# Moving a piece of layer 1, half of layer 2 and half of the dense part around the last tile's products in a recommender tower

## The chip, the cores and the metric

The kernel runs on one core of one Trainium2 chip. A core has TensorE (matmuls; PE in the profile, its weight loads PEld), VectorE (DVE), ScalarE (ACT), GpSimd (POOL) and SyncE (SP), and 16 DMA engines that all of them share. The metric is the time of one execution on the device in microseconds (us), the median of several runs: 106.18 us before, from 106.04 to 106.2 in 3 runs.

## What is computed

512 samples, 26 embedding tables with rows of 128 floats, and 128 dense features per sample. For each sample the 27 vectors (dense and 26 looked up) are multiplied with each other, the 351 products above the diagonal go with the dense features (twice) into a small network of three layers. All numbers are float32.

```
e = stack([tbl_f[ids[:, f]] for f in range(26)], axis=1)          # 512 x 26 x 128
x = concatenate([dense[:, None, :], e], axis=1)                   # 512 x 27 x 128
g = einsum('bnd,bmd->bnm', x, x)[:, triu_i, triu_j]               # 512 x 351
h = concatenate([dense, g, dense], axis=1)                        # 512 x 607
h = maximum(h @ W_top1 + b_top1, 0)                               # 512
h = maximum(h @ W_top2 + b_top2, 0)                               # 256
y = h @ W_top3                                                    # 1
```

## The kernel before

The samples are worked on in four tiles of 128. The order of the work on each engine is written out by hand, and each engine goes through its list in order and waits on semaphores; nothing is scheduled by a tool.

Eleven small tables are looked up by matmul with one-hot rows (`lookup`, L334): DVE and ACT make the one-hot rows and split the tables in two parts, and the table rows come by DMA from SP. The other 15 tables are gathered by POOL with indirect DMAs (L307), 15 for each tile in groups of 4, 4, 4 and 3, so 60 in all and groups 0 to 15. PE turns each group (`turn_group`, L349) into `ps_rows`, and ACT copies it into `xt` (`copy_group`, L659). The last group of the last tile is group 15. A gather waits, besides for the ring of rows, for lookups that are done (L306), the last of these waits being that for all 13 lookups.

A tile's products are `gram(t, quarter)` (L371): four quarters, each with 32 matmuls of 27x27 in the program. Every float32 matmul stands twice in the trace, each time as a weight load and a matmul, so that one quarter is 64 pairs of records, `layer1_pairs(t, m)` 6 pairs, half of `layer2` 8, half of `layer1_dense` 4. The first quarter waits until ACT has copied the tile's groups. After the last quarter DVE turns the blocks and packs them (`pack`, L587 and L592), PE turns the packed products (`turn_z`, `turn_last_z`), ACT copies them, and then come layer 1 (`layer1_pairs`, L420; of the last tile `layer1_last_pairs`, L397), relu on ACT and DVE, layer 2 (L434, L447), relu, and layer 3 (L460).

Tiles are overlapped: the quarters of tile 1 stand between pieces of layers 1 and 2 of tile 0, those of tile 2 between pieces of tile 1. Around the fourth tile (t = 3) the order is another: all of layer 1 of tile 2, the turn of group 14, half of layer 2 of tile 2, the turn of group 15 (the last turn), half of the dense part of tile 3 (L410), the four quarters in a row, and then the other half of layer 2 and of the dense part, while DVE packs.

The lines that matter are L512 to L540 of the list on PE, `gram` (L353), `layer1_pairs` (L413), `layer2` (L425), `layer1_dense` (L402), on ACT `relu1_low(2)`, `copy_group(14)` and `copy_group(15)` (L734 to L736).

Of the kernel before, what the change touches and what calls it, by code (L numbers as in the profile page):

```python
# [25 lines left out]
M1, M2 = H1 // P, H2 // P  # L26
# [95 lines left out]
def build(nc, dense_by_column, ids, ids_by_table, tables, w1, w2, columns, identity, out):  # L122
    with ExitStack() as ctx:
# [100 lines left out]
        def h1_block(t, m):  # L224

            return ps_a[:, m // 2, (m % 2) * P:(m % 2 + 1) * P]

        def h2_block(t, m):

            if t == TILES - 1:  # L230
                return ps_rows[:, m, 0:P]
            return ps_h2[:, 0, m * P:(m + 1) * P]
# [80 lines left out]
        def _(pe):  # L313
# [26 lines left out]
            def turn_group(g):  # L340

                t, first, n = GROUPS[g]
                if g >= 2:
                    pe.wait_ge(group_copied, g - 1)
                if g == 0:
                    pe.wait_ge(ident_landed, 16)
                pe.wait_ge(group_landed[g], 16 * n)
                for slot in range(n):
                    last = pe.transpose(ps_rows[:, g % 2, slot * P:(slot + 1) * P],  # L349
                                        rows_sb[:, t % ROWS_RING, first + slot, :], ident)  # L350
                last.then_inc(group_turned, 1)

            def gram(t, quarter):  # L353

                half, first = divmod(quarter * SPQ, SPB)
                if quarter == 0:

                    pe.wait_ge(group_copied, GROUPS_UP_TO[t])  # L360
                    pe.wait_ge(lookup_copied, FIRST_HALF_UP_TO if t < TILES // 2 else len(LOOKUPS))
                    if t == 0:
                        pe.wait_ge(dense_copied, 1)
                        pe.wait_ge(gram_zeroed, 1)
                    else:
                        pe.wait_ge(blocks_turned, t)
                for s in range(first, first + SPQ):
                    for j in range(P // NPAD):
                        b = t * P + j * NPAD + half * SPB + s
                        x = xt[:, b // RUN, :, b % RUN]  # L370
                        last = pe.matmul(ps_gram[j * NPAD:j * NPAD + N, half, s * N:(s + 1) * N], x, x,  # L371
                                         start=True, stop=True)
                if quarter == QUARTERS - 1:
                    last.then_inc(gram_done, 1)
# [27 lines left out]
            def layer1_dense(t, k):  # L402

                if k == 0 and t == 0:
                    pe.wait_ge(w1d_summed, 1)
                    pe.wait_ge(lookup_copied, len(LOOKUPS))
                if t:
                    pe.wait_ge(h1_high_ready if k else h1_low_ready, t)
                for m in range(2 * k, 2 * k + 2):
                    pe.matmul(h1_block(t, m), w1d[:, m * P:(m + 1) * P],  # L410
                              dense_sb[:, t * P:(t + 1) * P], start=(m % 2 == 0), stop=False, skip_group_check=True)

            def layer1_pairs(t, m):  # L413

                if m == 0:
                    if t == 0:
                        pe.wait_ge(w1_landed, 16)
                    pe.wait_ge(z_copied, t + 1)
                for c in range(ZC):
                    last = pe.matmul(h1_block(t, m), w1_sb[:, c, m * P:(m + 1) * P],  # L420
                                     zt[:, t % 2, c, :], start=False, stop=(c == ZC - 1), skip_group_check=True)
                if m % 2:
                    last.then_inc(h1_done, 1)

            def layer2(t, half):  # L425

                if half == 0:
                    pe.wait_ge(layers_landed, 32)
                    if t:
                        pe.wait_ge(h2_ready, M2 * t)  # L430
                pe.wait_ge(h1_high_ready if half else h1_low_ready, t + 1)
                for k in range(half * M1 // 2, (half + 1) * M1 // 2):
                    for m in range(M2):
                        last = pe.matmul(h2_block(t, m), w2_sb[:, k, m * P:(m + 1) * P], h1[:, t % 2, k, :],  # L434
                                         start=(k == 0 and m == 0), stop=(k == M1 - 1), skip_group_check=True)
                if half:
                    last.then_inc(h2_done, 1)
# [80 lines left out]
            turn_z(2)  # L518
            turn_group(13)

            for m in range(M1):
                layer1_pairs(2, m)
            turn_group(14)
            layer2(2, 0)
            turn_group(15)
            layer1_dense(3, 0)
            gram(3, 0)
            gram(3, 1)
            gram(3, 2)
            gram(3, 3)  # L530
            layer2(2, 1)
# [244 lines left out]
```

## Time and profile before

| | |
|---|---|
| median of 3 runs | 106.18 us (106.04 to 106.2) |
| span of the profiled execution | 141.4 us (the profile gives no other time for it) |
| PE busy | 105.4 us, 75% of the span |
| DVE, ACT, POOL busy | 52.7, 48.3, 60.9 us |
| "issue" in the chain that ended last | 23% of the span |
| mean granted TensorE clock | 0.855 of full speed |

The profiled execution is 35.2 us longer than the median of the runs. Most of that is idle time of PE that the profile puts down to "issue": the engine waited for nothing that the profile shows. It lies mainly between 51 and 99 us from the start of the span. From 102 us on the engine works at its pace, but for one gap.

In the rows below a timeline line is: start in us, length in us, engine, line of the kernel, operation, tile written <- tile read, form, number of records, and in brackets the idle time before them and what ended it. Lengths of matmuls are modelled at their end, so the difference of two starts is the better measure of a pace.

### The profile page before, as it was taken

Reading aid. Unit: us, or ns where it says so; the run is one execution under the profiler, and the core shown is the slowest. Engines: PE = TensorE matmul, PEld = TensorE weight load, DVE = VectorE, ACT = ScalarE, POOL = GpSimd, SP = SyncE. Lnnn points to the kernel's source line nnn. Section 1 sums busy time; section 2 is a strip of 40 time slices with the busy share of each in tenths; the row PEclk is TensorE's granted clock in tenths of the full one; section 3 lists DMA queues with packets and bytes.
Section 4 is the critical chain, followed back from the end, with each engine's and each line's share of the span. In section 5 each row is a group of like instructions: output and inputs, shape, how many; then the busy total and the mean of one; then the engine's idle time right before and its main releaser. Section 6 shows DMA issues by size and latency. Waiting matters only on the chain.

```text
span 141.4 us, 3474 instructions
## 1 busy us (share of the span) xinstructions
PE 105.4 (75%) x1525; PEld 85.9 (61%) x1525; DVE 52.7 (37%) x116; ACT 48.3 (34%) x82; POOL 60.9 (43%) x66
## 2 busy tenths in 40 slices
PE   6999899999979960366795223441997999967993
PEld 2476678788858950164684122221996998957980
DVE  2999999699279800000050000000043034103210
ACT  4749929597079520201023000000105106310342
POOL 1887877478567775705227777770000000000000
PEclk9999999999999997558689555555599999998699
DMA  4899999999992122100101122220000000000000
GB/s 131 282 234 256 264 262 234 249 241 234 305 381 71 51 60 55 38 19 23 37 5 48 48 59 57 56 56 19 0 5 5 5 5 0 0 5 5 5 0 1
DMA packets 5365, 13.46 MB, mean 95 GB/s; under 512 B 1731, under 2 KB 1991, under 8 KB 5222
## 3 DMA queue, kind: packets, MB, share of 16 engines
q1 hardware_dynamic: 3260, 9.11, 24.1%
q0 software_dynamic: 1920, 3.94, 10.8%
q8 instruction: 12, 0.20, 0.6%
q10 hardware_dynamic: 170, 0.18, 0.4%
q14 instruction: 3, 0.02, 0.0%
HBM read 13.23 MB, written 0.00 MB: 94 GB/s over the span
## 4 chain that ended last, share of the span: by engine, by line
PE 65%; issue 23%; DVE 6%; ACT 2%; DMA 2%; DVEq 0%
PE ps_a L334 27%; PE ps_gram L371 11%; PE ps_a L420 9%; DVE onehot L560 5%; PE ps_h L434 5%; PE ps_rows L349 4%; PE ps_a L410 3%; PE ps_a L397 2%; DMA idrow<-ids_by_table 2%; PE ps_rows L447 1%; ACT xt L659 1%; DVE part_sb L569 1%; PE ps_h L460 1%; ACT table_sb L666 1%; PE ps_gram L390 0%
## 5 line engine op out<-in xcount | busy, mean ns | idle before, releaser
L307 POOL DMA_INDIRECT rows_sb<-tbl,ids_sb x60 | 60.5, 1009 | 34.1 <-issue 16.5
L334 PE MATMUL ps_a<-onehot,part_sb 125*128 125x512 f32 (+1 forms) x208 | 46.9, 376 | 2.9 <-issue 2.6
L334 PEld LDWEIGHTS ps_a<-onehot,part_sb 125*128 125x128 f32 x208 | 35.8, 197 | 11.2 <-issue 3.4
L371 PE MATMUL ps_gram<-xt 128*27 128x27 f32 x1024 | 16.9, 205 | 22.5 <-issue 21.6
L371 PEld LDWEIGHTS ps_gram<-xt 128*27 128x27 f32 x1024 | 13.5, 118 | 27.1 <-issue 25.1
L560 DVE TENSOR_SCALAR onehot<-idrow,row_id 125x1024 fp32r<-125x1024 int16 (+1 forms) x42 | 27.7, 712 | 4.9 <-remote 3.3
L608 DVE TENSOR_SCALAR table_sb<-ps_a,columns_sb 128x128 f32<-128x128 f32 x8 | 2.4, 347 | 43.7 <-PE ps_a L420 39.5
L420 PE MATMUL ps_a<-table_sb,w_sb 128*128 128x128 f32 x72 | 13.0, 326 | 6.8 <-issue 6.4
L652 ACT COPY xt<-ps_a 128x512 f32<-128x512 f32 (+1 forms) x13 | 7.5, 575 | 31.1 <-PE ps_a L334 18.9
L587 DVE STREAM_TRANSPOSE table_sb<-ps_gram 128x864 f32<-128x864 f32 x4 | 4.3, 1084 | 32.3 <-PE ps_gram L371 32.3
L420 PEld LDWEIGHTS ps_a<-table_sb,w_sb 128*128 128x128 f32 x72 | 11.2, 232 | 7.6 <-issue 6.9
L569 DVE TENSOR_TENSOR part_sb<-table_sb,part_sb 125x512 fp32r<-125x512 f32 x22 | 14.5, 682 | 1.5 <-ACT part_sb L631 1.5
L631 ACT CAST part_sb<-table_sb 125x1024 fp32r<-125x1024 f32 (+1 forms) x12 | 11.7, 984 | 3.0 <-DMA table_sb<-tbl 2.9
L682 ACT ACTIVATE table_sb<-ps_a,columns_sb 128x128 f32<-128x128 f32 x8 | 2.5, 364 | 29.4 <-remote 23.5
L659 ACT COPY xt<-ps_rows 128x512 f32<-128x512 f32 (+1 forms) x16 | 9.7, 607 | 3.9 <-PE ps_rows L349 3.2
L349 PE MATMUL ps_rows<-ident_sb,rows_sb 128*128 128x128 f32 x60 | 9.2, 272 | 0.0
L689 ACT ACTIVATE table_sb<-ps_h,columns_sb 128x128 f32<-128x128 f32 x6 | 1.9, 364 | 17.9 <-PE ps_h L434 17.9
L349 PEld LDWEIGHTS ps_rows<-ident_sb,rows_sb 128*128 128x128 f32 x60 | 7.2, 140 | 0.8
L434 PE MATMUL ps_h<-table_sb,w_sb 128*128 128x128 f32 x48 | 7.5, 303 | 0.0
L641 ACT ACTIVATE distance<-idrow,row_id 125x1024 f32<-125x1024 int16 (+1 forms) x6 | 6.5, 1085 | 0.3 <-DMA idrow<-ids_by_table 0.3
L468 PE MATMUL ps_z<-zeros 128*128 128x512 bf16 x13 | 5.7, 629 | 1.2 <-DVE zeros L544 1.2
L434 PEld LDWEIGHTS ps_h<-table_sb,w_sb 128*128 128x128 f32 x48 | 6.3, 205 | 0.2
(35 smaller groups left out, 46.0 us busy)
## 6 DMA issues: line engine op xcount, KB each, us to landing
table_sb<-tbl SPq DMA_DIRECT2D x11, 448.0 KB
idrow<-ids_by_table SPq DMA_DIRECT2D x5, 256.0 KB
w_sb<-w SPq DMA_DIRECT2D x1, 1280.0 KB, 8.7
rows_sb<-tbl,ids_sb POOLq DMA_INDIRECT x60
table_sb<-tbl SPq DMA_DIRECT2D x10, 52.0 KB
w_sb<-w SPq DMA_DIRECT2D x1, 512.0 KB
dense_sb<-dense_by_column SPq DMA_DIRECT2D x1, 256.0 KB
idrow<-ids_by_table ACTq DMA_DIRECT2D x1, 128.0 KB
```

Source lines behind the costliest of these rows:

```text
L307: pool.indirect_dma_start(rows_sb[:, t % ROWS_RING, k, :], None, tables[f], bass.IndirectOffsetOnAxis(ids_sb[:, t, f:f + 1], 0),).then_inc ...
L334: last = pe.matmul(ps_a[:, i % 2, a:b], parts_sb[part][:, w, c * D:(c + 1) * D], unit_onehot(u, c)[:, member, a:b], start=(part == HIGH an ...
L349: last = pe.transpose(ps_rows[:, g % 2, slot * P:(slot + 1) * P], rows_sb[:, t % ROWS_RING, first + slot, :], ident)
L371: last = pe.matmul(ps_gram[j * NPAD:j * NPAD + N, half, s * N:(s + 1) * N], x, x, start=True, stop=True)
L420: last = pe.matmul(h1_block(t, m), w1_sb[:, c, m * P:(m + 1) * P], zt[:, t % 2, c, :], start=False, stop=(c == ZC - 1), skip_group_check=True)
L434: last = pe.matmul(h2_block(t, m), w2_sb[:, k, m * P:(m + 1) * P], h1[:, t % 2, k, :], start=(k == 0 and m == 0), stop=(k == M1 - 1), skip ...
L560: dve.tensor_scalar(unit_onehot(u, c), idrow[0:VP, w, 0:n, :], row_id[0:VP, first + c:first + c + 1], None, ALU.is_equal).then_inc(onehot_ ...
L569: dve.tensor_tensor(parts_sb[LOW][:, w, columns], table_sb[0:VP, s, columns], parts_sb[HIGH][:, w, columns].bitcast(F32), ALU.subtract).th ...
L631: act.copy(parts_sb[HIGH][:, w, first:end], table_sb[0:VP, s, first:end]).then_inc(part_ready[HIGH], 1)
L641: act.activation(distance[:, 0:n, :], idrow[0:VP, w, 0:n, :], ACT.Abs, bias=row_id[0:VP, negated:negated + 1]) \
L652: act.copy(xt[:, a // RUN:b // RUN, 1 + h, :], ps_a[:, i % 2, a:b].rearrange("p (q r) -> p q r", r=RUN)).then_inc(lookup_copied, 1)
L659: act.copy(xt[:, t * P // RUN:(t + 1) * P // RUN, slots, :].rearrange("p q n r -> p n q r"), ps_rows[:, g % 2, 0:n * P].rearrange("p (n q ...
```

## The change

The change reorders the list of PE and nothing else; ACT, DVE, POOL and SP go through the same instructions. Layer 1 of tile 2 is cut: its first two pieces stand where they were, the third stands between the turns of groups 14 and 15, and the fourth behind the last turn. The first half of layer 2 of tile 2 and of the dense part of tile 3 stand between the second and the third quarter of tile 3's products; they stood ahead of and behind the last turn.

```
-            for m in range(M1):
-                layer1_pairs(2, m)
+            layer1_pairs(2, 0)
+            layer1_pairs(2, 1)
             turn_group(14)
-            layer2(2, 0)
+            layer1_pairs(2, 2)
             turn_group(15)
-            layer1_dense(3, 0)
+            layer1_pairs(2, 3)
             gram(3, 0)
             gram(3, 1)
+            layer2(2, 0)
+            layer1_dense(3, 0)
             gram(3, 2)
             gram(3, 3)
             layer2(2, 1)
```

On PE, from the turn of group 13 to that of group 15 (L349: turns of a group; L420: layer 1 of tile 2, `w1_sb` its weights; counts are the program's, half of the trace's):

```order
 L349 MATMUL ps_rows<-ident_sb,rows_sb 128x128 x4
-L420 MATMUL ps_a<-table_sb,w1_sb 128x128 x12
+L420 MATMUL ps_a<-table_sb,w1_sb 128x128 x6
 L349 MATMUL ps_rows<-ident_sb,rows_sb 128x128 x4
+L420 MATMUL ps_a<-table_sb,w1_sb 128x128 x3
+L349 MATMUL ps_rows<-ident_sb,rows_sb 128x128 x3
+L420 MATMUL ps_a<-table_sb,w1_sb 128x128 x3
```

The last turn (x3) has 9 matmuls of layer 1 ahead of it instead of 12, and 3 behind it.

On PE, right behind these rows, the fourth tile's products (L371) with half of layer 2 (L434) and of the dense part (L410):

```order
+L371 MATMUL ps_gram<-xt 27x27 x64
 L434 MATMUL ps_h2<-table_sb,w2_sb 128x128 x4
-L349 MATMUL ps_rows<-ident_sb,rows_sb 128x128 x3
 L410 MATMUL ps_a<-dense_sb,w1d 128x128 x2
-L371 MATMUL ps_gram<-xt 27x27 x128
+L371 MATMUL ps_gram<-xt 27x27 x64
 L434 MATMUL ps_h2<-table_sb,w2_sb 128x128 x4
 L410 MATMUL ps_a<-dense_sb,w1d 128x128 x2
```

The 128 products stood in a row behind the last turn and the dense half; now the 4 + 2 matmuls stand in their middle, and none of the six stands ahead of the last turn or between it and the products.

## Rows read from the trace of the kernel before

**Rows 1.** The page: busy time, TensorE's granted clock in 40 slices, an instruction queue.

```profile
PE 105.4 (75%) x1525; PEld 85.9 (61%) x1525; DVE 52.7 (37%) x116; ACT 48.3 (34%) x82; POOL 60.9 (43%) x66
...
PEclk9999999999999997558689555555599999998699
...
q8 instruction: 12, 0.20, 0.6%
```

**Rows 2.** Waits of the whole span: us in total, times, longest us.

```profile
PE ps_gram L371 <- issue: 21.6, 20, 5.5
```

**Rows 3.** Timeline from layer 1 of tile 2 to the end of tile 3's products.

```profile
119.45 2.94 PE L420 MATMUL ps_a<-table_sb,w_sb 128*128 128x128 f32 x24 [0.28 <-ACT table_sb L666]
121.09 0.63 ACT L682 ACTIVATE table_sb<-ps_a,columns_sb 128x128 f32<-128x128 f32 x2 [1.18 <-PE ps_a L420]
...
122.67 1.06 PE L434 MATMUL ps_h<-table_sb,w_sb 128*128 128x128 f32 x8
...
123.56 0.49 PE L349 MATMUL ps_rows<-ident_sb,rows_sb 128*128 128x128 f32 x3
...
124.09 0.49 ACT L659 COPY xt<-ps_rows 128x384 f32<-128x384 f32 x1 [0.60 <-PE ps_rows L349]
...
124.64 1.47 PE L371 MATMUL ps_gram<-xt 128*27 128x27 f32 x151
...
128.22 1.09 PE L371 MATMUL ps_gram<-xt 128*27 128x27 f32 x105 [2.11 <-issue]
...
129.23 1.78 PE L434 MATMUL ps_h<-table_sb,w_sb 128*128 128x128 f32 x8
```

**Rows 4.** Stretches: us, busy time (records) by engine, clock, DMA share, GB/s.

```profile
125.70:126.70 1.00, 0.41 (x48) 0.30 (x35) 0.00 (x0) 0.00 (x0) 0.00 (x0) 1.00 0.06 16
126.70:128.20 1.50, 0.00 (x0) 0.00 (x0) 0.00 (x0) 0.00 (x0) 0.00 (x0) 1.00 0.00 0
...
129.20:130.60 1.40, 1.40 (x20) 1.37 (x9) 1.21 (x2) 0.00 (x0) 0.00 (x0) 0.64 0.06 12
```

**Rows 5.** Timeline of PE around tile 2's products.

```profile
99.95 2.71 PE L420 MATMUL ps_a<-table_sb,w_sb 128*128 128x128 f32 x12
...
106.92 0.60 PE L349 MATMUL ps_rows<-ident_sb,rows_sb 128*128 128x128 f32 x4
...
109.00 0.75 PE L371 MATMUL ps_gram<-xt 128*27 128x27 f32 x64 [0.77 <-ACT xt L659]
109.68 1.60 PE L420 MATMUL ps_a<-table_sb,w_sb 128*128 128x128 f32 x12
...
114.11 1.16 PE L434 MATMUL ps_h<-table_sb,w_sb 128*128 128x128 f32 x8
115.20 0.76 PE L371 MATMUL ps_gram<-xt 128*27 128x27 f32 x64
...
117.77 0.60 PE L349 MATMUL ps_rows<-ident_sb,rows_sb 128*128 128x128 f32 x4
```

**Rows 6.** Timeline of POOL: three of the 60 gathers.

```profile
50.93 0.95 POOL L307 DMA_INDIRECT rows_sb<-tbl,ids_sb  x1 [0.30 <-issue]
...
73.48 0.95 POOL L307 DMA_INDIRECT rows_sb<-tbl,ids_sb  x1 [5.49 <-PE ps_rows L349]
...
94.74 0.95 POOL L307 DMA_INDIRECT rows_sb<-tbl,ids_sb  x1 [0.30 <-issue]
```

**Rows 7.** Stretches behind the last gather, columns as in group 4.

```profile
96.00:97.00 1.00, 0.00 (x0) 0.12 (x1) 0.00 (x0) 0.00 (x0) 0.00 (x0) 0.50 0.29 66
97.00:98.00 1.00, 0.20 (x1) 0.00 (x0) 0.00 (x0) 0.00 (x0) 0.00 (x0) 0.50 0.00 0
```

**Rows 8.** Timeline of PE's weight loads, 48 to 75 us.

```profile
48.19 1.98 PEld L334 LDWEIGHTS ps_a<-onehot,part_sb 125*128 125x128 f32 x16
...
50.44 1.02 PEld L334 LDWEIGHTS ps_a<-onehot,part_sb 125*128 125x128 f32 x8
...
72.44 0.46 PEld L349 LDWEIGHTS ps_rows<-ident_sb,rows_sb 128*128 128x128 f32 x4
...
75.09 0.61 PEld L371 LDWEIGHTS ps_gram<-xt 128*27 128x27 f32 x41 [0.17 <-issue]
```

## The prediction, made before the change was run

> **What bounds the kernel now.** I read the page first, then the waits, the timeline of the last 40 us, the stretches around its one gap, and the timeline of POOL. PE is busy for 105.4 of 141.4 us [rows 1], about as long as a timed run (106.18 us) takes in all; PE sets the pace, unless what it waits for comes late. The first thing to see is that this profiled execution is no picture of a timed run: it is 35.2 us longer. PE idles 21.6 us ahead of products for "issue" alone [rows 2], and the clock row shows half speed over the same stretch [rows 1]. From 102 us on the pace is whole, so durations come from there, and the question becomes how PE and the gathers stand to each other in a run without those idles.
>
> The second thing is the gap in the fourth tile's products: 151 pairs of records from 124.64, then 2.11 us of nothing, then 105 pairs at full pace from 128.22 [rows 3]. A transfer of 16 GB/s over 1 us, about 16 KB, lies right ahead of the gap, and no other transfer until the next of that size behind it [rows 4]. The instruction queue of the page moved 0.20 MB in 12 packets [rows 1], 16 KB each. PE's 1525 weight loads and 1525 matmuls with some waits are about 3100 instructions, so a packet is about 256 of them, 128 pairs. I read the gap as PE running out of instructions: a block of 128 pairs ends at pair 151, so it began at pair 23, about 0.2 us into the products (124.86); the fetch of the next block starts about then and its instructions run at 128.22, 3.36 us later. The 128 products of the block need only 1.15 us (151 took 1.36), so PE stands for 2.2 us. Blocks that hold layer pieces last longer than the fetch, and no gap is seen there.
>
> The Trainium skill ("Runtime: NRT & Kernel Launch", Instruction fetch mechanics) says that such blocks are fetched ahead and that crossing a boundary is "mostly hidden". It agrees on the block; on the hiding the gap of 2.11 us speaks against it. By the rule there would be no gap in a timed run, which is a rival below.
>
> **The change part by part.** No instruction is added or taken away. All times here are from the start of tile 2's layer 1, T (119.45 in the profile).
>
> Before: the last turn starts at T + 4.1 (123.56). ACT copies group 15 from 124.09, and the products start at 124.64 = T + 5.19, 1.1 behind the turn's start [rows 3]. The 4 pairs of the dense half (0.45) fill part of that. The products end 4.6 later, of which 2.2 is the gap.
>
> After: the last turn has 18 pairs of layer 1 ahead (24 and 8 of layer 2 before). The 24 and 4 pairs of group 14's turn took 3.22 us (119.45 to 122.67), 0.115 each, and 8 of layer 2 took 0.89 (122.67 to 123.56) [rows 3]. So it could start 0.69 + 0.89, nearly 1.6, earlier, at T + 2.55. Behind it stand 6 pairs of layer 1, 0.69, instead of 4 of dense, 0.45. ACT's relu of tile 2 starts 1.64 after T and takes 0.63 [rows 3], then the copies of groups 14 and 15; that of 15 is ready when its turn is. The products still start about 1.1 to 1.2 behind the start of the turn: the copy ends there, and the layer-1 piece with its switch to the small matmuls ends there too. So the "piece behind the turn" is worth 0.0 to 0.1.
>
> The switch: 8 pairs of layer 2 ahead of products take 1.09 (114.11 to 115.20) [rows 5] and 0.89 ahead of large matmuls [rows 3]. One more such switch costs 0.2.
>
> The fetch: 12 pairs now stand behind half of the products instead of ahead of them, so the block begins at pair 35 of the products (0.3 us in, 0.1 later than before). Its 128 pairs are 93 products (0.84), the 8 + 4 pairs (0.89 + 0.45 + 0.2 for the switch) and 23 products (0.2): 2.6 us against 3.36. A gap of 0.8 is left in place of 2.2. Behind it 105 products remain, as before. So the end of the products is, in both kernels, the block's begin + 3.36 + 105 products. Only the begin moves. With the last turn free to move it moves by -1.56 + 0.1 + up to 0.15 (the start with its switch), so -1.3 us. The moved pieces are paid for wholly by the gap. What follows the products (DVE's pack, the last turns, layers 1 to 3) is the same and is not run by a block's end: its second fetch has the pack to hide behind.
>
> That -1.3 holds only if group 15 is there at T + 2.55. In the profile it is, since PE had lost over 30 us to POOL. In a timed run I work it out so:
>
> - Gathers: from 73.48 to 94.74 there are 18, 1.25 us each [rows 6]. From 50.93 on there are 28; with no wait for PE (the wait for all lookups would be met) the last starts at 50.93 + 27 x 1.25 = 84.7. Its data land some 2.3 later (94.74 to 97.0, where the traffic stops [rows 6, 7]), at 87.0.
> - PE: from 50.44 [rows 8] four lots of 8 lookups at 1.0, four quarters of 0.68 (109.00 to 109.68 [rows 5]), three switches of 0.2 and one fetch gap of about 1.0 where two quarters stand together give 58.7. Then 2.65 to tile 1's products (72.44 to 75.09 [rows 8]), 8.77 + 2.08 to tile 2's (109.00 to 117.77 and 106.92 to 109.00 [rows 5]) and 10.45 to T (109.00 to 119.45): T = 82.7.
>
> So group 15 lands at T + 4.3. Before, PE is at the last turn at T + 4.1 and waits 0.2. After, it is there at T + 2.55 and waits 1.75, and behind this wait are queued the last piece of layer 1 and all products, then the two halves that used to be done ahead. Group 14, four gathers earlier less one (3 x 1.25), lands at T + 0.6, ahead of its turn at T + 1.4. The end of the products then hangs on group 15 in both kernels: turn, copy and 1.15, block begin (0.1 later after), 3.36, 105 products. Sum for the likeliest case: +0.1 (block begin) +0.04 (switch at the start) - 0 = +0.14, less 0.0 to 0.2 if group 15 comes a little before T + 4.1. I take +0.12: 106.3 us. Counted against the profiled execution it would be 141.4 - 1.3, since there the gathers are long done; I carry differences, not its span, to 106.18. As a check, 87.0 + 1.1 + 16.7 (products to the end, 124.64 to 141.4) = 104.8, 1.4 short of the median, which is the error of this reconstruction, nearly as large as the 1.75 us of waiting that it says.
>
> Bounds of what the trace doesn't show. Gather pace in a timed run: 0.95 (no issue time) to 1.33; at 0.95 the last lands 8 us sooner and the change gets its -1.3; I take 1.25, the row. Fetch: from 1.15 (no gap) to 3.36; I take 3.36. Clock: 12 pairs of layer 1 take 2.71 at half and 1.60 at full clock [rows 5]; the stretch behind the gap is at 0.64 of full [rows 4], so an idle of 2 us brings some half speed. The change trades one idle for another; from -1.2 (the half speed behind the products goes) to +1.2 (it falls on the layer pieces); I take 0.
>
> **The rivals.**
>
> PE is late, not the gathers. If in a timed run PE reaches T about 1.8 us later than I worked out (or the gathers come sooner), group 15 is there at T + 2.55 and the whole -1.3 arrives: 104.9 us; with the half-speed stretch behind a smaller gap gone too, down to 104. For it: the 1.4 us that my sum is short of the median may be PE's. Against it: the rows' pace of both. Values in between give a part of the gain.
>
> The fetch is short or hidden in a timed run, with the gathers as worked out. Then the halves between the quarters hide nothing and are work that stood in the wait for group 15. It decides from a fetch under 2.6 us: at 1.8 (the transfer ends about 1.8 behind the block's begin [rows 4]) the after loses 0.8 + 0.14, 107.1 us; with no gap at all 1.54 + 0.14, 107.9. For it: less traffic without a profile; against: nothing else moved during the gap. The skill's "mostly hidden" is this case.
>
> Half speed falls on the pieces in the middle. The wait for group 15 grows from 0.2 to 1.75 us, and with a clock at half behind it the block takes 0.84 x 1.9 + 1.54 x 1.7 + 0.2, about 4.4 instead of 2.6, 1.0 over the fetch: 107.3. For it: half speed behind the 2.11 us gap. Against: before has the longer gap and pays behind it.
>
> **How the numbers follow.** Waiting for group 15 with the long fetch: 0.43, 106.3 (own range 106.0 to 106.7). PE late: 0.33, 104.9. Short fetch: 0.14, 106.8 to 107.9. Half speed: 0.10, 107.3. A measurement of this kernel tells 0.2%, 0.2 us, from nothing. Faster: 0.33 and 0.06 of the first case, 0.39. Same: 0.30. Slower: 0.14 + 0.10 and 0.07 of the first, 0.31. The range for 8 in 10 leaves out the lowest clock gains and the hidden fetch: 104.7 to 107.2.
>
> **What would show it.** In the profile after, the gap must lie about 23 products into the third quarter and be 0.8 us long instead of 2.1 at pair 151; the span should fall by 1.3 there if idles elsewhere are equal, with ACT's copy of group 15 starting 2.5 to 3.2 us behind T. If timed runs then gain as much, the gathers are not the bound. If the gap sits elsewhere, my reading of blocks is wrong. If the time grows by 0.8 or more with the gap smaller, the short fetch or the clock row decides which of the last two it was.

## The result, and the profile after

The changed kernel took 102.96 us (median of 4 runs, 102.78 to 103.59) against 106.12 for the kernel before (4 runs, 106.04 to 106.2): a ratio of 0.9715, 95% interval 0.9666 to 0.9764. Two later comparisons of the same pair, on two chips (a1 and a2 below), gave 0.9859 (0.9801 to 0.9916) and 0.9846 (0.9792 to 0.9900). The gain is there in all three, and by these ratios the later two show about half of the first. A ratio here leaves out the executions that lie over 1.5% above the fastest of the same kernel, and with them many of those in which TensorE's clock fell, while the medians are of all executions: by these the two later ones are 0.985 and 0.979. The prediction was no change in the likeliest case (106.3), with 104.7 as its lower end: wrong.

The profiled execution this time had none of the long idles of the one before: a span of 101.2 us at a time of 103.07, so that 1.9 us of the time lie outside the span. The page after, busy time and clock (the rows that answer to [rows 1]):

```profile
PE 94.3 (93%) x1525; PEld 77.4 (77%) x1525; DVE 52.8 (52%) x116; ACT 48.3 (48%) x82; POOL 60.6 (60%) x66
...
PEclk9999999999999999999999999999999999999999
```

The timeline after, from layer 1 of tile 2 to the last tile's turns (it answers to [rows 3]):

```profile
81.82 1.61 PE L420 MATMUL ps_a<-table_sb,w_sb 128*128 128x128 f32 x12 [0.27 <-ACT table_sb L668]
...
84.37 0.49 PE L349 MATMUL ps_rows<-ident_sb,rows_sb 128*128 128x128 f32 x3
...
84.69 0.83 PE L420 MATMUL ps_a<-table_sb,w_sb 128*128 128x128 f32 x6
84.89 0.50 ACT L661 COPY xt<-ps_rows 128x384 f32<-128x384 f32 x1 [0.28 <-PE ps_rows L349]
...
85.46 1.28 PE L371 MATMUL ps_gram<-xt 128*27 128x27 f32 x128
...
86.67 1.16 PE L434 MATMUL ps_h<-table_sb,w_sb 128*128 128x128 f32 x8
...
87.66 0.61 PE L410 MATMUL ps_a<-dense_sb,w1d 128*128 128x128 f32 x4
...
88.20 0.37 PE L371 MATMUL ps_gram<-xt 128*27 128x27 f32 x23
...
89.12 1.09 PE L371 MATMUL ps_gram<-xt 128*27 128x27 f32 x105 [0.55 <-issue]
...
90.14 1.16 PE L434 MATMUL ps_h<-table_sb,w_sb 128*128 128x128 f32 x8
```

T, the start of tile 2's layer 1, is 81.82. The last turn starts at T + 2.55, the products at T + 3.64 (T + 5.19 before [rows 3]), and the gap is where it was said to be, 23 products into the third quarter, 0.55 us long instead of 2.11. The last turn waits for nothing. POOL's last gather, and the traffic behind it (columns as in [rows 4]; the engines are PE, PEld, DVE, ACT, POOL):

```profile
81.04 0.94 POOL L307 DMA_INDIRECT rows_sb<-tbl,ids_sb  x1 [0.30 <-issue]
```

```profile
82.70:83.40 0.70, 0.70 (x9) 0.70 (x8) 0.00 (x0) 0.00 (x0) 0.00 (x0) 1.00 0.29 76
83.40:84.00 0.60, 0.60 (x8) 0.60 (x7) 0.00 (x0) 0.54 (x3) 0.00 (x0) 1.00 0.00 0
```

The data of group 15 are in at 83.4, T + 1.6, a full microsecond ahead of its turn. The prediction had T + 4.3.

### The profile page after: what moved, and what is told of

Its sections match the earlier page's. It is cut to its first block, busy times and chain, and to the rows that moved or that the text cites. A ratio compares the mean times of both kernels' runs of the same rounds, so it can differ in the third digit from the quotient of the medians.

```text
span 101.2 us, 3474 instructions
## 1 busy us (share of the span) xinstructions
PE 94.3 (93%) x1525; PEld 77.4 (77%) x1525; DVE 52.8 (52%) x116; ACT 48.3 (48%) x82; POOL 60.6 (60%) x66
## 4 chain that ended last, share of the span: by engine, by line
PE 71%; DVE 18%; DMA 3%; issue 3%; ACT 3%; DVEq 0%
PE ps_a L334 29%; PE ps_gram L371 12%; DVE onehot L562 12%; PE ps_a L420 9%; PE ps_rows L349 6%; PE ps_h L434 5%; DVE part_sb L571 4%; PE ps_a L410 3%; DMA idrow<-ids_by_table 3%; PE ps_a L397 3%; PE ps_rows L447 2%; DVE table_sb L589 1%; ACT xt L661 1%; PE ps_h L460 1%; DVE z L594 1%
## 5 line engine op out<-in xcount | busy, mean ns | idle before, releaser
L334 PE MATMUL ps_a<-onehot,part_sb 125*128 125x512 f32 (+1 forms) x208 | 45.2, 367 | 0.8 <-DVE part_sb L571 0.5
L334 PEld LDWEIGHTS ps_a<-onehot,part_sb 125*128 125x128 f32 x208 | 34.1, 188 | 8.6 <-DVE part_sb L571 2.4
L371 PE MATMUL ps_gram<-xt 128*27 128x27 f32 x1024 | 13.2, 195 | 2.0 <-issue 1.1
L371 PEld LDWEIGHTS ps_gram<-xt 128*27 128x27 f32 x1024 | 11.0, 108 | 4.6 <-issue 1.5
L420 PE MATMUL ps_a<-table_sb,w_sb 128*128 128x128 f32 x72 | 9.7, 283 | 0.3 <-ACT table_sb L668 0.3
L349 PE MATMUL ps_rows<-ident_sb,rows_sb 128*128 128x128 f32 x60 | 9.2, 272 | 0.0
L420 PEld LDWEIGHTS ps_a<-table_sb,w_sb 128*128 128x128 f32 x72 | 8.6, 192 | 0.7 <-ACT table_sb L668 0.5
L349 PEld LDWEIGHTS ps_rows<-ident_sb,rows_sb 128*128 128x128 f32 x60 | 7.2, 141 | 0.8
L434 PE MATMUL ps_h<-table_sb,w_sb 128*128 128x128 f32 x48 | 7.0, 288 | 0.0
L468 PE MATMUL ps_z<-zeros 128*128 128x512 bf16 x13 | 5.2, 588 | 1.2 <-DVE zeros L546 1.2
L648 ACT ACTIVATE onehot<-distance 125x1024 fp32r<-125x1024 f32 (+1 forms) x6 | 5.9, 991 | 0.4
```

Of the source, the lines that this page charges most:

```text
L334: last = pe.matmul(ps_a[:, i % 2, a:b], parts_sb[part][:, w, c * D:(c + 1) * D], unit_onehot(u, c)[:, member, a:b], start=(part == HIGH an ...
```

## The experiments

### The kernel before, four more times

No edit. These are profiles without the long idles of the first (span 141.4 us).

> The kernel before, unchanged, for a profile of it without the long idles. Theory (instruction fetch, gathers early): span about 104.3, group 15's last gather issued near 81 us, the gap of 2.1 to 2.2 us at pair 151 of the fourth tile's products, and half the clock behind it; ratio 1.00. Rival (the gathers bound the kernel before): POOL's last data land behind PE's arrival at the last turn, and PE idles ahead of that turn by 0.2 us or more.

> One more look at the kernel before, for its clock behind the gap. Theory (in a part of its executions the clock falls to half behind the 2.1 to 2.7 us gap, at a price of 1.0 us from the restart of the products to the end: 13.1 instead of 12.1 us): either of the two, and the stretch from the restart to the end is 13.1 with half clock and 12.1 without. Rival (the spread of the times comes from ahead of tile 2's layer 1): restart to end 12.1 in all looks.

> As b1: a further look at the kernel before; half clock behind the gap and 13.1 us from the restart to the end, or full clock and 12.1 us.

> As b1: a further look at the kernel before; half clock behind the gap and 13.1 us from the restart to the end, or full clock and 12.1 us.

Ratio of the first to the kernel before 1.0013 (0.9972 to 1.0054). The four profiles have none of the long idles, at times of 105.07, 105.7, 106.23 and 105.72; they are called clean below. Timeline of b0, from tile 2's layer 1 to the restart of the products, with the last gather of POOL below:

```profile
81.94 2.94 PE L420 MATMUL ps_a<-table_sb,w_sb 128*128 128x128 f32 x24 [0.28 <-ACT table_sb L666]
...
86.05 0.49 PE L349 MATMUL ps_rows<-ident_sb,rows_sb 128*128 128x128 f32 x3
...
87.12 1.47 PE L371 MATMUL ps_gram<-xt 128*27 128x27 f32 x151
91.12 1.09 PE L371 MATMUL ps_gram<-xt 128*27 128x27 f32 x105 [2.53 <-issue]
```

```profile
81.21 0.94 POOL L307 DMA_INDIRECT rows_sb<-tbl,ids_sb  x1 [0.30 <-issue]
```

The gap of 2.53 us behind product 151 is there in an execution without long idles, so it belongs to the timed runs. The last gather starts at 81.21 also here, far ahead of the last turn at 86.05: gathers bound neither kernel. That settles the rival of b0. Its theory had two things otherwise: the gap is longer than the 2.1 to 2.2 us expected (2.0 to 2.6 in the four), and in b0 no half clock follows it.

The clock behind the gap comes in two kinds. Stretches from the restart of the products to the end, b1 first, then b0, then the changed kernel (PE's granted clock is the third number from the right):

```profile
90.73:103.88 13.15, 10.70 (x176) 9.19 (x176) 2.72 (x12) 3.71 (x13) 0.00 (x0) 0.87 0.01 3
```

```profile
91.12:103.18 12.06, 9.48 (x176) 7.82 (x176) 2.72 (x12) 3.77 (x13) 0.00 (x0) 1.00 0.01 3
```

```profile
89.12:101.18 12.06, 9.48 (x176) 7.82 (x176) 2.72 (x12) 3.77 (x13) 0.00 (x0) 1.00 0.01 3
```

The same 176 pairs and 12 DVE instructions take 13.15 us where part of them ran at half clock (1.2 instead of 2.4 GHz; mean 0.87 of full) and 12.06 where none did. What the engine did before is the same in both: 151 products, over 2.5 us of nothing, 105 products. In b1 this is what it costs right behind the gap:

```profile
90.73 1.09 PE L371 MATMUL ps_gram<-xt 128*27 128x27 f32 x105 [2.62 <-issue]
91.75 1.67 PE L434 MATMUL ps_h<-table_sb,w_sb 128*128 128x128 f32 x8
93.21 1.06 PE L410 MATMUL ps_a<-dense_sb,w1d 128*128 128x128 f32 x4
...
94.84 3.31 PE L397 MATMUL ps_a<-table_sb,w_sb 128*128 128x128 f32 x24
```

(8 of layer 2 took 1.16, 4 of dense 0.61 and the 24 of layer 1 2.85 after the change.) The rival, that the spread comes only from ahead of T, falls, though there is spread there as well: T lies between 81.46 and 83.2 in the clean profiles of both kernels.

Each timed run of the experiments also has its mean granted clock. It is 0.984 in b1 and b2, whose traces have half clock in one stretch, behind the gap, and 1.0 in b0 and b3, which have none. Over all executions of the order before that have one, 40 of 66 show 0.984, and take 106.19 us on average; the other 26 show 0.999 or 1.0 and take 105.34. That the other 38 of the 40 lost their clock at the same place is inferred from the same mean. Of the changed kernel's 16 in three comparisons none shows less than 1.0; they take 103.45 on average.

All profiles of the experiments in one table (us; "begin" is the weight load with which the block that ends at the gap begins, of pair 24 of the products, in after, a1, a2 and p1 of pair 36 and in v1 of pair 42; "restart" is behind the gap, in v1 the first pair of the next block; the first line is the profile with the long idles):

| kernel | products start | begin | restart | begin to restart | restart to end |
|---|---|---|---|---|---|
| before, first | T + 5.19 | T + 5.34 | T + 8.77 | 3.43 | 13.15 (half clock) |
| b0 | T + 5.19 | T + 5.34 | T + 9.19 | 3.85 | 12.06 |
| b1 | T + 5.19 | T + 5.34 | T + 9.27 | 3.93 | 13.15 (half clock) |
| b2 | T + 5.19 | T + 5.34 | T + 9.03 | 3.68 | 13.13 (half clock) |
| b3 | T + 5.19 | T + 5.34 | T + 8.70 | 3.36 | 12.08 |
| after | T + 3.64 | T + 3.93 | T + 7.30 | 3.38 | 12.06 |
| a1 | T + 3.64 | T + 3.92 | T + 6.93 | 3.00 | 12.07 |
| a2 | T + 3.64 | T + 3.93 | T + 7.48 | 3.55 | 12.07 |
| p1 | T + 4.46 | T + 4.76 | T + 8.02 | 3.26 | 12.07 |
| p2 | T + 4.98 | T + 5.13 | T + 8.73 | 3.59 | 12.08 |
| f1 | T + 5.19 | T + 5.34 | T + 8.75 | 3.41 | 12.23 |
| v1 | T + 3.13 | T + 3.47 | (T + 6.86) | no gap | 12.06 |

### One half of the change at a time

p1 puts only the halves of layer 2 and dense between the quarters:

```
             for m in range(M1):
                 layer1_pairs(2, m)
             turn_group(14)
-            layer2(2, 0)
             turn_group(15)
-            layer1_dense(3, 0)
             gram(3, 0)
             gram(3, 1)
+            layer2(2, 0)
+            layer1_dense(3, 0)
             gram(3, 2)
             gram(3, 3)
```

> Of the change only the halves of layer 2 and of the dense part between the quarters; layer 1 of tile 2 stays in one piece ahead of the turns of groups 14 and 15. Fetch theory: the products start 0.8 us later than in the changed kernel, as nothing covers ACT's copy of group 15; their gap is 0.6 to 0.8 us at product 151, the clock stays full; 103.7 to 104.0 us. Rival (the piece behind the last turn makes most of the gain): no less than 105 us.

Measured 104.09 (10 runs), ratio 0.9909 (0.9859 to 0.996). As expected, the products start 0.8 later than after the whole change, for want of a cover for ACT's copy; the gap is 0.43 us and the time 104.09, a little under and a little over what was expected. None of its 10 runs lost the clock, yet six lie near 104.0 and four near 105.1; what parts them was not looked into.

p2 does only the cut of layer 1; the last turn comes as early as in the whole change, and the halves of layer 2 and dense stand between it and the products:

```
-            for m in range(M1):
-                layer1_pairs(2, m)
+            layer1_pairs(2, 0)
+            layer1_pairs(2, 1)
             turn_group(14)
-            layer2(2, 0)
+            layer1_pairs(2, 2)
             turn_group(15)
+            layer1_pairs(2, 3)
+            layer2(2, 0)
             layer1_dense(3, 0)
```

> Of the change only the cut of layer 1 with its last piece behind the last turn; the halves of layer 2 and of the dense part stand ahead of the four quarters in a row. Fetch theory: ACT's copy is covered (0.1 to 0.3 us), the gap of 2.2 us stays and the half clock behind it: 105.8 to 106.1 us. Rival (the earlier last turn is what gains): 104 us or less.

Measured 105.66, ratio 0.9922 (0.9861 to 0.9983; one run of 111 us, with the clock at 0.845, is in the median). The products start 0.2 earlier than in the order before, the gap is 2.28 us, and 6 of 10 runs lost the clock. Alone, the piece is worth the 0.2 of a covered copy, and an earlier last turn gains nothing more. The medians of p1 and p2 stand 1.6 us apart: what matters is what stands in the gap. In the whole change the piece lets the products start 0.8 earlier (p1 against after), as there nothing else covers the copy.

### Work of no use in the gap

f1 leaves the order before and adds 8 matmuls of zeros between the second and the third quarter; f2 adds 11.

```
             gram(3, 1)
+            for _ in range(8):
+                pe.matmul(ps_z[:, 0, :], zeros[:, 0:P], zeros[:, :], start=True, stop=True)
             gram(3, 2)
```

> The order before, with 8 matmuls of zeros (128x512, bf16, 0.22 us each, results unused) between the second and third quarter of the fourth tile's products. They add work and move no other. Fetch theory: the products end where they did or 0.1 us later, since the 1.7 us stand in the gap, of which 0.4 is left. Clock: with the idle gone the clock stays full behind the products, and the time falls by 1 to 1.8 us, to 104.3 to 105.1. Rival (the clock behind the gap costs a timed run nothing, and all 3 us come from moved work): 106.1 to 106.3. Rival (no fetch; the gap is not in timed runs): 107.8.

> As the run with the idle filled, but 11 matmuls of zeros (2.4 us), so that next to nothing is left of the gap. Fetch theory: products end within 0.3 us of where they do before. Theory that half clock behind the gap makes the rest: the time falls on average by 0.5 to 1.1 us against the kernel before, in spite of 11 more matmuls. Rival (no clock effect in timed runs): +0.1 to +0.5 us.

f1: 105.4 (10 runs), ratio 0.995 (0.9903 to 0.9997), where 104.3 to 105.1 was expected: less than that. Its timeline:

```profile
87.19 1.28 PE L371 MATMUL ps_gram<-xt 128*27 128x27 f32 x128
88.41 1.90 PE L530 MATMUL ps_z<-zeros 128*128 128x512 bf16 x8
90.24 0.31 PE L371 MATMUL ps_gram<-xt 128*27 128x27 f32 x15
90.75 1.15 PE L371 MATMUL ps_gram<-xt 128*27 128x27 f32 x113 [0.20 <-issue]
```

The 0.20 us of gap that are left stand behind product 143, again 151 pairs from the first product. 1.8 us of extra work end within the old gap (restart at T + 8.75, among the values of the order before), and the time doesn't grow: the engine had been waiting there for something that is not its own work. No run of f1 is at 0.984, against 29 of 41 of the order before on the same chip. So the idle brings the half clock, and keeping PE busy through it, with work of no use, avoids it. The gain is only 0.6 since the fall comes in a part of the executions, and since on this chip those with it average only 0.6 more than those without (106.16 and 105.57; on the other two chips 0.6 and 1.45 more). f1's own average, 105.50, is that of the order before at full clock.

f2: 106.46 (6 runs), ratio 1.0061 (0.9987 to 1.0135), its median 1.0 us above the order before, more than even its rival gave. No run is at 0.984, and the products end at T + 10.1, as in the order before (9.7 to 10.3). But behind them comes a new gap, ahead of the last turns:

```profile
91.58 1.28 PE L371 MATMUL ps_gram<-xt 128*27 128x27 f32 x128
...
93.79 0.61 PE L410 MATMUL ps_a<-dense_sb,w1d 128*128 128x128 f32 x4
95.22 0.30 PE L390 MATMUL ps_z<-ident_sb,z 128*128 128x128 f32 x1 [0.82 <-DVE z L594]
```

The profile puts the 0.82 us down to DVE, which had packed the first part 0.8 us before (in b0 the turn starts 0.43 us behind the start of that packing, here 1.19). A block boundary fits better: pair 151 from the first product is now 12 products into the third quarter, which PE passed at 91.66, and pair 279 (256 products, 11 zeros, 8 and 4 pairs) is right ahead of this turn, 3.6 us later. With no gap in the products the next block was used up before its own fetch was through. The run says nothing on the clock's price.

### The block boundary moved

s1 is the order before with 20 tiny matmuls at the very front:

```
                 pe.matmul(ps_z[:, 0, :], zeros[:, 0:P], zeros[:, :], start=True, stop=True)
+            for _ in range(20):
+                pe.matmul(ps_z[:, 0, 0:32], zeros[:, 0:P], zeros[:, 0:32], start=True, stop=True)
```

> The order before, with 20 tiny matmuls (32 columns, of zeros) added behind the warm-up, while the tables are still on their way. Nothing near the end is touched, but every later instruction stands 20 pairs further on. Fetch theory: the gap in the fourth tile's products comes 20 pairs earlier, behind product 131 instead of 151, as long as before; the end of the products is 0.0 to 0.2 us earlier (the block begins 0.2 us earlier and 20 more products stand behind the gap); time 0.0 to 0.5 us from the kernel before. Rival (the gap comes from the products themselves, a queue or a limit of theirs that fills): it stays behind product 151.

The gap did not come behind product 131, nor did it stay at 151:

```profile
87.07 2.51 PE L371 MATMUL ps_gram<-xt 128*27 128x27 f32 x256
89.50 0.60 PE L434 MATMUL ps_h<-table_sb,w_sb 128*128 128x128 f32 x3
92.04 0.82 PE L434 MATMUL ps_h<-table_sb,w_sb 128*128 128x128 f32 x5 [1.94 <-issue]
```

All 256 products run without a break, and PE stands behind the third pair of layer 2, 259 pairs from the first product: 131 + 128, one block further on. Both theories' places are wrong, and the rival's (the products themselves choke something at 151) is refuted by 256 in a row. The fetch theory is mended by the windows of the same profile, with the two transfers of 16 KB:

```profile
85.80:86.90 1.10, 1.10 (x11) 0.93 (x9) 0.00 (x0) 0.50 (x2) 0.00 (x0) 1.00 0.05 15
86.90:89.30 2.40, 2.26 (x247) 2.18 (x250) 0.00 (x0) 0.11 (x1) 0.00 (x0) 1.00 0.00 0
89.30:90.60 1.30, 0.80 (x35) 0.57 (x23) 0.97 (x1) 0.00 (x0) 0.00 (x0) 1.00 0.06 13
90.60:92.00 1.40, 0.00 (x0) 0.00 (x0) 1.13 (x10) 0.00 (x0) 0.00 (x0) 1.00 0.00 0
```

With the boundary 3 products in, the first transfer starts about 1.2 us before the first product, while PE works ahead of it; in the kernel before, with the boundary at 23, it comes about 1.1 us into the products [rows 3, 4]. So the fetch can go ahead of PE's execution, and here it went far enough that no gap came. At the next boundary of s1 the transfer starts 1.1 us behind PE's passing, as it does around here in the other profiles (0.7 to 1.5). That the early one has to do with the wait for ACT's copy, which stands just ahead of that boundary, is a guess from one case and was not tried. The time: 106.11 (4 runs, 104.25 to 107.87), ratio 0.9939 (0.9858 to 1.0021), undecided; two runs at full clock took 104.5 on average and two with half clock 107.6. That is 3 us between the two, more than a fall behind one gap costs, and is not explained.

### The changed kernel again, and a step further

> The changed kernel once more, beside the kernel before and the next two on one chip. Theory (block begin 1.3 to 1.5 us earlier, and half clock behind the gap in a part of the executions of the kernel before): 103.0 us, 2.0 to 3.1 below the kernel before, and no half clock in its profile. Rival (the first 3.0 us were an accident of that chip): a ratio of 0.985 or more.

> The changed kernel a third time, beside the kernel before. Block theory alone: ratio 0.982 to 0.988 (1.3 to 1.9 us). With half clock in most executions of the kernel before: 0.97 to 0.98.

a1: 103.84 (6 runs), ratio 0.9859; it was to be 103.0 and falls on the side of its rival, by which a part of the first 3 us was an accident. a2: 103.4 (6 runs), ratio 0.9846, within what the gap alone was to give, as the ratio leaves out most of the half clock; by medians it is 0.979. Averages of all executions part the two causes better. On the chip of a1 the order before takes 105.46, at full clock 105.23, and the changed kernel 103.70: 1.5 us for the gap and 0.2 for the clock, which fell in 4 of 11 runs. On the chip of a2 they are 105.76, 105.03 and 103.46: 1.6 and 0.7, with 7 of 14. On the chip of the first experiments it fell in 29 of 41. In the first comparison the four runs of the kernel before lay within 0.2 us at 106.1, where the average with half clock is 106.19; their clock is not known, so that they all had it is likely and not shown. It would put 0.85 us of the 3.2 down to the clock, and leave 2.3 to the gap, 0.7 more than in the later two; that much stays unexplained.

v1 goes on in the same way:

```
             turn_group(14)
-            layer1_pairs(2, 2)
             turn_group(15)
-            layer1_pairs(2, 3)
+            layer1_pairs(2, 2)
             gram(3, 0)
             gram(3, 1)
+            layer1_pairs(2, 3)
             layer2(2, 0)
...
-            relu1_low(2)
             copy_group(14)
             copy_group(15)
+            relu1_low(2)
```

> The changed kernel taken further: group 15 turned right behind group 14, layer 1's last piece of tile 2 between the second and the third quarter as well, and ACT copies groups 14 and 15 ahead of tile 2's first relu. Fetch theory: the products start at T + 3.2 instead of T + 3.63 (T: start of tile 2's layer 1), the gap shrinks from 0.66 to under 0.2, the products end 0.3 to 0.4 us earlier: 102.6 us where the changed kernel takes 103.0. Gather rival: group 15 (data in at T + 1.5) is now late for its turn at T + 1.8 and PE idles ahead of it by over 0.3 us; no gain.

Measured 103.25 (6 runs) beside 103.84 for the changed kernel on the same chip; ratio to the kernel before 0.9788 (0.9727 to 0.9849) against 0.9859. It was to be 102.6. The intervals overlap, so which of the two is faster is not shown by the times. The trace:

```profile
84.22 0.94 PE L349 MATMUL ps_rows<-ident_sb,rows_sb 128*128 128x128 f32 x7
85.00 0.83 PE L420 MATMUL ps_a<-table_sb,w_sb 128*128 128x128 f32 x6
85.91 1.28 PE L371 MATMUL ps_gram<-xt 128*27 128x27 f32 x128
87.12 0.94 PE L420 MATMUL ps_a<-table_sb,w_sb 128*128 128x128 f32 x6
...
89.33 1.40 PE L371 MATMUL ps_gram<-xt 128*27 128x27 f32 x128
90.65 1.16 PE L434 MATMUL ps_h<-table_sb,w_sb 128*128 128x128 f32 x8
```

T is 82.78 here, and the products end at T + 7.87, against T + 8.32 in the first profile after, 7.95 in a1 and 8.49 in a2: earlier than all three, but than a1's by less than these differ among themselves. The products start at T + 3.13, and no gap is left. Even with its turn right behind that of group 14, group 15 is there in time, against the gather rival.

## Why the prediction was wrong, by its own steps

- **The gap is a fetch of instructions** (begin + 3.36, then 105 products). Right. It lies in timed runs too; it follows the position of the block (with 8 foreign pairs ahead of it, it stands behind product 143 in f1, and a gap came back 128 pairs further on in s1 and in f2); foreign work fits into it (f1). Sizes: begin to restart is 3.0 to 3.9 us, mean 3.65 in five profiles of before and 3.31 in three after; I had one value, 3.36.
- **The moved begin, -1.3 us with the turn free.** Right in kind: T + 5.34 to T + 3.93, -1.41.
- **The piece behind the last turn, 0.0 to 0.1.** It was counted against the dense half that used to be the cover. As such it holds (the products start 1.08 us behind the turn's start before and 1.09 after), but without it the halves leave the copy uncovered: 0.8 (p1).
- **"So group 15 lands at T + 4.3."** This step failed, and with it the likeliest case: the 1.75 us of waiting for group 15 that ate the -1.3 were 0. T was 81.46 to 83.2 where I had 82.7: fair. The landing was at 83.4 where I had 87.0. I took POOL's place from the disturbed profile (the first, with the long idles) at 50.93, believing that all before 51 us was sound. It was not: in the profile after the gather that stands at 50.93 [rows 6] starts at 47.25, 27 gathers ahead of the last; the disturbed one shows two waits of POOL of about 2 us earlier that the one after doesn't have (below). PE's eight lookups of [rows 8] were late as well, but by half as much (50.44 against 48.58). A difference of two places, each read from a disturbed trace, carried the error of both. The check against the total was misread: 104.8 is a span, and with the 1.9 us outside the span it stands for 106.7, 0.5 over the median and not 1.4 short of it. It could not have shown the error in any case, for by PE's branch the sum is 82.7 + 21.95 (T to the end in the profile), 104.65, nearly the same.

```profile
26.48 1.11 POOL L307 DMA_INDIRECT rows_sb<-tbl,ids_sb  x1 [2.15 <-remote]
...
39.77 1.41 POOL L307 DMA_INDIRECT rows_sb<-tbl,ids_sb  x1 [1.98 <-remote]
```

- **Clock: from -1.2 to +1.2, "I take 0".** This term failed as well: with the gathers in time and the clock at 0 the sum was 104.9, still inside the range, and what lies below it is in part the clock. The direction could have been read: the gap was to shrink to 0.8, and from 102 us on half clock came behind the 2.11 us gap only [rows 1, 4]. It is worth 1.07 us where it falls (13.13 against 12.06 from the restart to the end), and it falls in 40 of 66 executions of the order before and in 0 of 16 after.
- **The sum.** In the profiles: begin -1.41, fetch -0.34 (3.31 against 3.65, within its spread), clock -1.07 x 3/5 = -0.64: -2.4 from T to the end. In the timed runs of the two comparisons that have a clock, the averages fell by 1.75 (a1's chip) and 2.30 (a2's), and in the first comparison by 3.05. The sum lies among these; it is not confirmed to better than that, and the fetch's -0.34 may be chance.
- **The rivals.** "PE is late, not the gathers" is what came true, though by what it had in brackets: PE was on time and the gathers early. Its times (104.9, with the clock 104) were still above the 102.96 to 103.84 measured. The short fetch (107.1 to 107.9) and the half speed in the middle (107.3) did not occur. The Trainium skill's rule ("Runtime: NRT & Kernel Launch", Instruction fetch mechanics) that a boundary's fetch is mostly hidden holds for blocks with layer pieces, and not for 128 products in 1.15 us: the clean gaps are 2.0 to 2.6 us.

## What to carry to other kernels

Where TensorE runs hundreds of tiny matmuls in a row, look for gaps marked "issue" that lie a fixed number of instructions apart with a 16 KB transfer ahead of them: the cure is to spread large matmuls among the small ones, and the worth is how much earlier the small ones begin. Count with such a gap the clock that may fall behind it. And from a profile that is much longer than the timed runs take durations, but no positions of engines against each other; a second profile of the unchanged kernel would have shown the true ones.

## What the runs showed of the hardware

- A block of 256 instructions (16 KB) took 3.0 to 3.9 us from PE's passing the boundary before it to its first instruction; the transfer's own share is about 1 us.
- In the last two tiles' products the transfer of the next block mostly started 0.7 to 1.5 us behind PE's passing a boundary; in s1 it once started 1.2 us ahead. So 20 harmless instructions at the front of a program moved a 2 us gap from one place to another near its end. What lets it start early is not shown.
- In five profiles of the order before PE is without work for 2.0 to 2.6 us at the gap, and in three of them the granted clock then goes from 2.4 to 1.2 GHz; by the mean clock the same holds for 40 of 66 executions of this order. With a gap of 0.2 to 0.7 us (four profiles) it fell in none of the 26 executions of after and p1.
- Two quarters of the products (64 pairs each), near each other and both at full clock, took 0.91 and 0.68 us from their start to the next work, here in the profile after (tile 2's first two quarters):

```profile
70.92 0.97 PE L371 MATMUL ps_gram<-xt 128*27 128x27 f32 x64 [0.78 <-ACT xt L661]
71.83 1.60 PE L420 MATMUL ps_a<-table_sb,w_sb 128*128 128x128 f32 x12
73.36 0.75 PE L371 MATMUL ps_gram<-xt 128*27 128x27 f32 x64
74.04 1.60 PE L420 MATMUL ps_a<-table_sb,w_sb 128*128 128x128 f32 x12
```

What picks the pace was not looked into; it may be part of the spread of the times.
